# Output projection two steps later, in the batch's own bank, and both rope parts together

## The chip, the cores and the metric

One NeuronCore of one Trainium2 chip. The metric is device time in microseconds of one launch; the kernel before was timed in three runs.

## The reference

Sixteen batches of 128 tokens, 256 features. First cross-attention with 32 heads of 8 features, then a mixture-of-experts block. Cut to what matters here:

```
xn   = layernorm(x)
q    = rope(xn @ Wq, pos);  k = rope(ctx @ Wk, pos);  v = ctx @ Wv     # rope: x1*cos - x2*sin, x1*sin + x2*cos
w    = softmax(q k^T / sqrt(8)) per head                               # 128 x 128 per head
x    = x + (w v) @ Wout + bout
x    = x + moe(layernorm(x))                                           # router, 32 experts, shared expert
```

## The kernel before

Each engine has its own hand-written queue of instructions, and semaphores tie them together. The attention stage is software-pipelined over batches: every engine runs a function `period(b)` for b from -3 to 16 (`periods`, L239; ten of them, b = 2 to 11, in a loop of five turns with two periods in each), and a period has eight steps g = 0 to 7, one for each group of four heads ("quad"). In period b the engines work on batch b and also on b+1, b+2, b+3 (earlier stages) and on b-1, called `o` (the last stages). In the code `m1 = b+1`, `m3 = b+3` and so on. "Batch b" below, of a period, means period(b).

What happens to a batch, in the order of the data:

- `transpose_xc`, `project_k`, `project_q` (TensorE, steps 0 to 2 of the period three earlier) put queries and keys into bank M1. VectorE applies rope: `rope_cos` (L472) multiplies by the cosines, `rope_sin` (L479) by the sines in two instructions. GpSimd adds the two and splits the result into two half-precision parts (`split`). `transpose_k` and `transpose_q` turn them; ScalarE copies them out.
- `logits_q` (L583): one quad of scores with queries on the partitions, into one of two banks SB. VectorE takes the row maximum (`row_max`, L487). After each two quads `transpose_max` (L593) turns the maxima, VectorE copies them (`evac_max`, L494), and a DMA of SyncE writes them into spare rows of `qst` (L309). It is there three steps later that they are needed.
- `logits_k` (L597): the same scores with keys on the partitions and the maximum subtracted by the matmul; on every second step it waits for that DMA. ScalarE takes the exponential (L384). SyncE also copies the keys (`kz`, L302) once ScalarE has done the previous batch's last exponential, ahead of the first DMA of maxima of the period in its queue.
- `weigh_values` (L608): multiplies with the values, into the batch's output bank `OB[par]` (par is the batch's parity). Quads 0 to 3 run at step 4 of the batch's own period, quads 4 to 7 at step 0 of the next.
- In the next period: ScalarE copies the outputs (`evac_OT`, step 2), TensorE turns them (`transpose_outputs`, step 3), VectorE divides by the sums (`normalise`, L500, step 3), TensorE turns the result (`transpose_attn`, L626, step 4) into the right half of bank M0, ScalarE copies it (L412, step 5), TensorE multiplies with Wout (`project_out`, L633, step 6) into the left half of M0, and VectorE adds it to X (L516, step 7) and takes the statistics for the second norm (L529).

Bank M0 is shared: `project_v` and `transpose_q` of later batches write it too, and so `project_v` waits for the X add of an earlier batch and `transpose_attn` waits until the queries are copied out.

At the attention stage's end ScalarE and VectorE also split the shared expert's weights into two parts (L162 in period 14, step 7; L166 in period 15, step 7). During the loop ScalarE issues loads of expert weights, at steps 1, 4 and 6.

Of the kernel before, what the change touches and what calls it, by code (L numbers as in the profile page):

```python
# [26 lines left out]
ALU = mybir.AluOpType  # L27
# [144 lines left out]
def attention(nc, sem, X, identf, st2, ring, ahead, x, ctx_in, pos, wq, wkv, wout, bout):  # L172
    with ExitStack() as es:
# [65 lines left out]
        def periods(eng, period):  # L239

            for n in range(-3, 2):
                period(Batch(n // 2, n % 2))
            with eng.Fori(0, 5) as i:
                for u in range(2):
                    period(Batch(i, 2 + u))
            for n in range(12, NB + 1):
                period(Batch(n // 2, n % 2))

        def inside(b, lo=0, hi=NB - 1):

            return not isinstance(b.n, int) or lo <= b.n <= hi
# [102 lines left out]
        def _(act):  # L356
# [21 lines left out]
            def period(b):  # L378
                m1, m2, m3, m4, o = b + 1, b + 2, b + 3, b + 4, b + -1
                for g in range(QUADS):  # L380
# [26 lines left out]
                    if g == 7 and isinstance(b.n, int) and b.n == 14:  # L407
                        ahead.split_hi(act, raw_wsg)
                    if g == 5 and inside(o):
                        act.wait_ge(attnT_mm, o.n + 1)  # L410
                        at_least(act, wo_mm, o.n)
                        act.copy(attnT[:, :, :], M0[:, D:2 * D].rearrange("p (c t) -> p c t", c=DK)).then_inc(attnT_ok, 1)  # L412
                    if g == 6 and inside(m2):
# [13 lines left out]
        def _(dve):  # L427
# [82 lines left out]
            def period(b):  # L510
                m1, m3, o = b + 1, b + 3, b + -1
                for g in range(QUADS):
                    if g == 7 and inside(o):
                        dve.wait_ge(wo_mm, o.n + 1)
                        dve.wait_ge(x_biased, o.n + 1)
                        dve.tensor_tensor(X[:, o.n, :], M0[:, 0:D], X[:, o.n, :], ALU.add).then_inc(x1_ok, 1)  # L516
                    if g == 3 and inside(m3):
                        rope_cos(m3)
                    if g % 2 == 1:
                        who, half = (b, (g + 3) // 2) if g < 5 else (m1, (g - 5) // 2)  # L520
                        if inside(who):
                            evac_max(who, half)
                    who, u = (b, g + 5) if g < 3 else (m1, g - 3)
                    if inside(who):
                        row_max(who, u)
                    if g == 7 and inside(o):
                        dve.wait_ge(x1_ok, o.n + 1)
                        dve.wait_ge(rope_tab, 3)
                        dve.bn_stats(st2[:, o.n, :], X[:, o.n, :]).then_inc(st2_ok, 1)  # L529
                    if g == 3 and inside(o):  # L530
                        normalise(o)
                    if g == 4 and inside(m3):
                        rope_sin(m3)
                    if g == 4 and isinstance(b.n, int) and b.n == -3:
                        split(dve, m3)
                    if g == 4 and isinstance(b.n, int) and b.n == -2:
                        statistics(4, NB, 1)
                    if g == 7 and isinstance(b.n, int) and b.n == 15:
                        ahead.split_lo(dve, raw_wsg)
# [4 lines left out]
        def _(pe):  # L544
# [34 lines left out]
            def project_v(m):  # L579
                at_least(pe, x1_ok, m.n - 2)  # L580
                pe.matmul(M0[:, 0:D], xcT[m.par][:, DK, :], WKV[:, D:2 * D], start=True, stop=True).then_inc(v_mm, 1)
# [26 lines left out]
            def weigh_values(m, g):  # L608
                pe.wait_ge(exp_ok, QUADS * m.n + g + 1)
                if g == 0:  # L610
                    at_least(pe, v_ok, m.n + 1)
                    at_least(pe, attn_ok, m.n - 1)
                for j in range(4):
# [12 lines left out]
            def transpose_attn(m):  # L626
                pe.wait_ge(attn_ok, m.n + 1)
                pe.wait_ge(qst_ok, min(m.n + 3, NB) if isinstance(m.n, int) else m.n + 3)
                for c in range(DK):
                    ins = pe.transpose(M0[:, D + c * P:D + c * P + P], attn[:, c * P:c * P + P], identf[:, :])  # L630
                ins.then_inc(attnT_mm, 1)

            def project_out(m):  # L633
                pe.wait_ge(attnT_ok, m.n + 1)
                for c in range(DK):
                    ins = pe.matmul(M0[:, 0:D], attnT[:, c, :], WO[:, c, :], start=(c == 0), stop=(c == DK - 1))
                ins.then_inc(wo_mm, 1)
# [3 lines left out]
            def period(b):  # L641
                m1, m2, m3, o = b + 1, b + 2, b + 3, b + -1
                for g in range(QUADS):
# [9 lines left out]
                    if g == 0 and inside(m1):  # L653
                        project_v(m1)
                    if g == 0 and inside(o):
                        for q in range(4, QUADS):
                            weigh_values(o, q)
# [11 lines left out]
                    if g == 3 and inside(o):  # L669
                        transpose_outputs(o)  # L670
                    if g == 4 and inside(o):
                        transpose_attn(o)
                    if g == 5 and inside(m2):
                        transpose_k(m2)
                    if g == 6 and inside(o):
                        project_out(o)
            periods(pe, period)
# [621 lines left out]
```

## Time and profile before

| | us |
|---|---|
| median of three runs (lowest, highest) | 409.04 (405.89, 412.06) |
| the profiled execution | 406.55 |
| its span, first to last instruction | 404.8 |
| busy in the span: TensorE matmul / weight load | 311.9 / 209.2 |
| busy: VectorE, ScalarE, GpSimd | 218.0, 194.0, 165.5 |
| attention stage, about | 0 to 219.7 |

The page cuts the span into 40 slices of about 10 us; the attention stage is the first 22. Times in the rows below are microseconds from the first instruction. Matmuls are pipelined: a row's length reaches past the point at which the next may start, so work on TensorE is best measured from one start to the next.

### The profile page before, as it was taken

The numbers are of one execution on the slowest core, as the hardware profiler recorded it, in microseconds if no ns is written. First come the engines' busy times: TensorE is split into PE (matmuls) and PEld (weight loads), VectorE is DVE, ScalarE is ACT, GpSimd is POOL, SyncE is SP. The second block draws the span as 40 slices with busy tenths as digits, with TensorE's granted clock in tenths as the row PEclk, the third lists the DMA queues.
The fourth block names the chain that finished last, engine by engine and source line by source line (L and its number), as shares of the span: only waits on it lengthen the run. The fifth ranks groups of instructions, "written<-read, shape, count | busy, mean of one in ns | idle before, by whom it ended". The sixth has DMA issues, their size and how long they took to land. (4 is left out here: it accounts for less than half of the span.)

```text
span 404.8 us, 9209 instructions
## 1 busy us (share of the span) xinstructions
PE 311.9 (77%) x2986; PEld 209.2 (52%) x2986; DVE 218.0 (54%) x598; ACT 194.0 (48%) x370; POOL 165.5 (41%) x249
## 2 busy tenths in 40 slices
PE   0668999999999999999884879789888995864000
PEld 0446777767676777776562334546467442331000
DVE  4495777777776777777655358996114321111000
ACT  3136786777677776776663745432324221110000
POOL 4453444433344444332002002545872245777620
PEclk9986999999999999999997599999999999895555
DMA  6311114444355344432100361111337793222265
GB/s 186 133 33 35 36 52 116 126 123 117 107 135 140 102 129 127 130 73 86 42 2 0 132 225 71 28 52 59 98 101 220 219 274 52 24 28 27 25 111 105
DMA packets 35035, 39.27 MB, mean 97 GB/s; under 512 B 8032, under 2 KB 29120, under 8 KB 34752
## 3 DMA queue, kind: packets, MB, share of 16 engines
q1 hardware_dynamic: 24082, 21.55, 18.4%
q10 hardware_dynamic: 8030, 11.93, 10.4%
q0 software_dynamic: 2896, 5.44, 8.0%
q8 instruction: 15, 0.25, 0.2%
q14 instruction: 12, 0.10, 0.1%
HBM read 26.36 MB, written 10.32 MB: 91 GB/s over the span
## 5 line engine op out<-in xcount | busy, mean ns | idle before, releaser
L384 ACT ACTIVATE pw<-bank 128x512 f32<-128x512 f32 x128 | 76.7, 600 | 45.4 <-PE bank L615 34.2
L491 DVE TENSOR_REDUCE mx<-bank 128x4 f16<-128x512 f32 x128 | 87.2, 684 | 16.2 <-PE bank L591 15.4
L261 POOL TENSOR_TENSOR rot<-t 128x256 f32<-128x256 f32 x30 | 21.2, 726 | 93.3 <-DVE t L484 93.3
L604 PE MATMUL bank<-qst,kz 128*128 128x128 f16 x512 | 50.0, 221 | 4.0 <-DMA qst<-mxs 3.3
L591 PE MATMUL bank<-kz,qst 128*128 128x512 f16 x128 | 49.5, 388 | 1.5 <-issue 0.9
L604 PEld LDWEIGHTS bank<-qst,kz 128*128 128x128 f16 x512 | 37.4, 99 | 16.7 <-DMA qst<-mxs 5.3
L615 PE MATMUL bank<-pw,V 128*32 128x128 f32 x1024 | 34.7, 276 | 0.0
L893 POOL DMA_INDIRECT out<-ac,dst x16 | 21.7, 1355 | 27.4 <-DVE ac L1116 10.4
L1173 PE MATMUL mbank<-hT,WSG 128*128 128x512 f16 (+1 forms) x144 | 31.9, 379 | 0.0
L1116 DVE TENSOR_SCALAR ac<-mbank,wpair 128x256 f32<-128x256 f32 x16 | 7.7, 484 | 43.4 <-DMA odd<-ac,dst 40.5
L615 PEld LDWEIGHTS bank<-pw,V 128*32 128x32 f32 x1024 | 25.9, 109 | 9.0 <-issue 7.4
L1185 PE MATMUL mbank<-WSD,ac 128*128 128x256 f32 (+1 forms) x96 | 21.9, 382 | 5.8 <-POOL ac L852 4.4
L498 DVE COPY mxs<-bank 8x128 f16<-8x128 f16 x64 | 13.2, 206 | 23.7 <-PE bank L595 23.7
L852 POOL TENSOR_TENSOR ac<-ac,sg 128x512 f32<-128x512 f32 (+1 forms) x9 | 11.8, 1317 | 34.2 <-ACT ac L933 34.1
L893 POOL DMA_INDIRECT odd<-ac,dst x16 | 21.7, 1354 | 8.1 <-DVE ac L1116 5.9
L1173 PEld LDWEIGHTS mbank<-hT,WSG 128*128 128x128 f16 (+1 forms) x144 | 15.1, 106 | 15.6 <-ACT ac L933 0.4
L1185 PEld LDWEIGHTS mbank<-WSD,ac 128*128 128x128 f32 (+1 forms) x96 | 17.9, 189 | 9.6 <-POOL ac L852 5.4
L272 POOL TENSOR_TENSOR tokst<-rot,tokst 128x256 f16<-128x256 f32 x30 | 20.2, 672 | 4.4
L417 ACT COPY kT<-bank 128x1024 f16<-128x1024 f16 x16 | 16.2, 1011 | 9.8 <-PE bank L576 8.7
L1242 PE MATMUL mbank<-ring_gu,xbT 128*64 128x352 f32 x112 | 18.9, 460 | 0.8 <-ACT xbT L791 0.8
L972 ACT ACTIVATE ac<-mbank 128x176 f32<-128x176 f32 x16 | 5.1, 318 | 29.7 <-PE mbank L1242 27.9
L562 PE MATMUL bank<-WQ,xcT 128*128 128x256 f32 x64 | 18.8, 422 | 0.0
(174 smaller groups left out, 597.3 us busy)
## 6 DMA issues: line engine op xcount, KB each, us to landing
ring_gu<-in_L_ffn_w_gate_up ACTq DMA_DIRECT2D x20, 352.0 KB
kz<-kT SPq DMA_DIRECT2D x64, 64.0 KB, 2.0
ring_dn<-in_L_ffn_w_down ACTq DMA_DIRECT2D x10, 352.0 KB
ring_gu<-in_L_ffn_w_gate_up SPq DMA_DIRECT2D x8, 352.0 KB
X<-in_x SPq DMA_DIRECT2D x4, 512.0 KB, 7.4
table<-ac SPq DMA_DIRECT2D x8, 256.0 KB, 2.2
odd<-zero SPq DMA_DIRECT2D x1, 2048.0 KB, 7.2
out<-X SPq DMA_DIRECT2D x4, 512.0 KB
```

The lines of the kernel that those rows point to most:

```text
L261: eng.tensor_tensor(rot[:, part], t1[:, part], t2[:, part], ALU.add).then_inc(rot_ok[w], 1)
L272: eng.tensor_tensor(tokst[m.par][:, w, :, a:a + HD], r, hi, ALU.subtract)
L384: act.activation(pw[g % 4][:, :], STB[g % 2][:, :], ACT.Exp, scale=SCALE).then_inc(exp_ok, 1)
L491: dve.tensor_reduce(mx[u // 2 % 2][:, u % 2:8:2], SB[u % 2][:, :].rearrange("p (j t) -> p j t", j=4), axis=AX.X, op=ALU.max, negate=True). ...
L562: ins = pe.matmul(M1[:, 0:D], xcT[m.par][:, c, :], WQ[:, c, :], start=(c == 0), stop=(c == DK - 1))
L591: pe.matmul(SB[u % 2][:, :], qst[m.par][:, u, :], kz[m.par][:, :, u, :], start=True, stop=True).then_inc(s_mm, 1)
L604: ins = pe.matmul(STB[g % 2][:, j * P:j * P + P], kz[m.par][:, j, g, :], qst[m.par][:, g, :], start=True, stop=True)
L615: ins = pe.matmul(OB[m.par][32 * j:32 * j + 32, (g % 4) * P:(g % 4) * P + P], V[m.par][:, a:a + SLOT], pw[g % 4][:, j * P:j * P + P], star ...
L893: pool.indirect_dma_start(to[:, :], bass.IndirectOffsetOnAxis(ap=dst[:, 2 * k + w:2 * k + w + 1], axis=0), ys[k % 3][rows, :], None, compu ...
L1173: ins = pe.matmul(GU[2 * (i % 2) + w][0:n, :], WSG[:, c, u, w * SHARED + a:w * SHARED + a + n], hT[:, v, c, 512 * k:512 * k + 512], start= ...
L1185: ins = pe.matmul(DN[m % 2][:, 0:D], ac[k % 2][0:n, f, j * P:j * P + P], WSD[0:n, f, :], start=(f == 0), stop=(f == 2))
L1242: ins = pe.matmul(EB[k % 3][lane, 0:2 * INNER], xbT[:, c, e * CAP:e * CAP + LANE], ring.gu[place][:, e % 2, c, :], start=(c == 0), stop=(c ...
```

## The change

- VectorE: `rope_cos` and `rope_sin` run one behind the other at step 3, after that step's copy of maxima and row maximum. Before, the cosine part came ahead of both and the sine part at the end of step 4.
- VectorE: `normalise` moves from step 3 to step 5.
- TensorE: `transpose_attn` moves from step 4 to step 6, ScalarE's copy of it from step 5 to 7, `project_out` from step 6 to step 0 of the next period, the X add with the statistics from step 7 to step 2 of the next. They write and read the batch's own output bank and no longer M0.
- Waits: `transpose_attn` no longer waits for the copied queries; `project_v` waits for the queries and no longer for the X add; the first `weigh_values` of a batch waits for the X add of the batch two before, where it waited for that batch's normalise.
- One more period (b = 17) runs, for the last batch.

```diff
-            for n in range(12, NB + 1):
+            for n in range(12, NB + 2):
                 period(Batch(n // 2, n % 2))
...
-                    if g == 5 and inside(o):
+                    if g == 7 and inside(o):
                         act.wait_ge(attnT_mm, o.n + 1)
                         at_least(act, wo_mm, o.n)
-                        act.copy(attnT[:, :, :], M0[:, D:2 * D].rearrange("p (c t) -> p c t", c=DK)).then_inc(attnT_ok, 1)
+                        act.copy(attnT[:, :, :], OB[o.par][:, D:2 * D].rearrange("p (c t) -> p c t", c=DK)).then_inc(attnT_ok, 1)
...
             def period(b):
-                m1, m3, o = b + 1, b + 3, b + -1
+                m1, m3, o, o2 = b + 1, b + 3, b + -1, b + -2
                 for g in range(QUADS):
-                    if g == 7 and inside(o):
-                        dve.wait_ge(wo_mm, o.n + 1)
-                        dve.wait_ge(x_biased, o.n + 1)
-                        dve.tensor_tensor(X[:, o.n, :], M0[:, 0:D], X[:, o.n, :], ALU.add).then_inc(x1_ok, 1)
-                    if g == 3 and inside(m3):
-                        rope_cos(m3)
                     if g % 2 == 1:
...
                         row_max(who, u)
-                    if g == 7 and inside(o):
-                        dve.wait_ge(x1_ok, o.n + 1)
+                    if g == 2 and inside(o2):
+                        dve.wait_ge(wo_mm, o2.n + 1)
+                        dve.wait_ge(x_biased, o2.n + 1)
+                        dve.tensor_tensor(X[:, o2.n, :], OB[o2.par][:, 0:D], X[:, o2.n, :], ALU.add).then_inc(x1_ok, 1)
+                        dve.wait_ge(x1_ok, o2.n + 1)
                         dve.wait_ge(rope_tab, 3)
-                        dve.bn_stats(st2[:, o.n, :], X[:, o.n, :]).then_inc(st2_ok, 1)
-                    if g == 3 and inside(o):
+                        dve.bn_stats(st2[:, o2.n, :], X[:, o2.n, :]).then_inc(st2_ok, 1)
+                    if g == 3 and inside(m3):
+                        rope_cos(m3)
+                        rope_sin(m3)
+                    if g == 5 and inside(o):
                         normalise(o)
-                    if g == 4 and inside(m3):
-                        rope_sin(m3)
...
             def project_v(m):
-                at_least(pe, x1_ok, m.n - 2)
+                at_least(pe, qst_ok, m.n)
...
                 if g == 0:
                     at_least(pe, v_ok, m.n + 1)
-                    at_least(pe, attn_ok, m.n - 1)
+                    at_least(pe, x1_ok, m.n - 1)
...
             def transpose_attn(m):
                 pe.wait_ge(attn_ok, m.n + 1)
-                pe.wait_ge(qst_ok, min(m.n + 3, NB) if isinstance(m.n, int) else m.n + 3)
                 for c in range(DK):
-                    ins = pe.transpose(M0[:, D + c * P:D + c * P + P], attn[:, c * P:c * P + P], identf[:, :])
+                    ins = pe.transpose(OB[m.par][:, D + c * P:D + c * P + P], attn[:, c * P:c * P + P], identf[:, :])
...
-                    ins = pe.matmul(M0[:, 0:D], attnT[:, c, :], WO[:, c, :], start=(c == 0), stop=(c == DK - 1))
+                    ins = pe.matmul(OB[m.par][:, 0:D], attnT[:, c, :], WO[:, c, :], start=(c == 0), stop=(c == DK - 1))
...
+                    if g == 0 and inside(o2):
+                        project_out(o2)
                     if g == 0 and inside(o):
                         for q in range(4, QUADS):
                             weigh_values(o, q)
...
-                    if g == 4 and inside(o):
-                        transpose_attn(o)
                     if g == 5 and inside(m2):
                         transpose_k(m2)
                     if g == 6 and inside(o):
-                        project_out(o)
+                        transpose_attn(o)
```

## Rows read from the trace of the kernel before

**Rows 1.** Busy time by stretch, batch 6's period: us and (instructions) of each engine.

```profile
102.01:113.79 11.78, 11.00 (x147) 8.46 (x146) 8.44 (x20) 8.44 (x15) 4.99 (x10) 1.00 0.43 113
```

**Rows 2.** Timeline, TensorE, period 6: start, length, engine, line, operation, [idle before].

```profile
101.56 0.39 PE L604 MATMUL bank<-qst,kz 128*128 128x128 f16 x4 [0.17 <-issue]
...
108.51 0.40 PE L604 MATMUL bank<-qst,kz 128*128 128x128 f16 x4 [0.74 <-DMA qst<-mxs]
...
110.57 0.22 PE L595 MATMUL bank<-identh,mx 128*128 128x128 f16 x1
...
112.65 0.39 PE L604 MATMUL bank<-qst,kz 128*128 128x128 f16 x4
...
113.14 0.39 PE L604 MATMUL bank<-qst,kz 128*128 128x128 f16 x4
```

**Rows 3.** Timeline, TensorE, period 7, up to the next period's first logits.

```profile
117.36 0.38 PE L591 MATMUL bank<-kz,qst 128*128 128x512 f16 x1
...
121.09 0.43 PE L630 MATMUL bank<-identf,attn 128*128 128x128 f32 x2
...
121.61 0.23 PE L595 MATMUL bank<-identh,mx 128*128 128x128 f16 x1
...
122.27 0.62 PE L576 MATMUL bank<-identh,tokst 128*128 128x128 f16 x8 [0.19 <-DVE t L484]
...
123.17 1.03 PE L636 MATMUL bank<-WO,attnT 128*128 128x256 f32 x4
...
124.03 0.39 PE L604 MATMUL bank<-qst,kz 128*128 128x128 f16 x4
...
124.85 0.39 PE L604 MATMUL bank<-qst,kz 128*128 128x128 f16 x4 [0.17 <-issue]
```

**Rows 4.** Timeline, SyncE's queue, period 6: key copy and first DMA of maxima.

```profile
102.64 2.46 SPq L302 DMA_DIRECT2D kz<-kT  x4
...
105.24 0.59 SPq L309 DMA_DIRECT2D qst<-mxs  x1
```

**Rows 5.** Timeline, VectorE: a copy of period 6, then period 7.

```profile
110.92 0.21 DVE L498 COPY mxs<-bank 8x128 f16<-8x128 f16 x1 [0.40 <-PE bank L595]
...
117.78 0.69 DVE L491 TENSOR_REDUCE mx<-bank 128x4 f16<-128x512 f32 x1 [0.61 <-PE bank L591]
...
118.75 0.69 DVE L477 TENSOR_TENSOR t<-bank,RC 128x512 f32<-128x512 f32 x1 [0.28 <-PE bank L562]
...
119.36 0.20 DVE L498 COPY mxs<-bank 8x128 f16<-8x128 f16 x1
...
120.53 0.42 DVE L507 TENSOR_TENSOR attn<-bank,rec 128x256 f32<-128x256 f32 x1
...
120.87 0.68 DVE L491 TENSOR_REDUCE mx<-bank 128x4 f16<-128x512 f32 x1
...
121.47 0.75 DVE L484 TENSOR_TENSOR t<-bank,RS 128x256 f32<-128x256 f32 x2
```

**Rows 6.** Timeline, period 8: DMA of maxima and the logits that waited for it.

```profile
134.28 0.53 SPq L309 DMA_DIRECT2D qst<-mxs  x1
...
136.38 0.40 PE L604 MATMUL bank<-qst,kz 128*128 128x128 f16 x4
```

**Rows 7.** Timeline, end of the attention stage.

```profile
204.41 1.37 ACT L162 ACTIVATE WSG<-raw_wsg 128x1408 f16<-128x1408 f32 x1
...
212.60 1.18 PE L615 MATMUL bank<-pw,V 128*32 128x128 f32 x32
...
212.71 0.60 ACT L384 ACTIVATE pw<-bank 128x512 f32<-128x512 f32 x1 [0.94 <-PE bank L604]
...
213.85 0.59 ACT L422 COPY OT<-bank 128x512 f32<-128x512 f32 x1 [0.55 <-PE bank L615]
```

**Rows 8.** Line L581 (project_v): what TensorE waited for before it (nothing), and who waited.

```profile
its engine sat idle before it (us, times) until:
who waited for it (us, times):
```

More of the change, by code:

```diff
@@ L641, in period @@
             def period(b):
-                m1, m2, m3, o = b + 1, b + 2, b + 3, b + -1
+                m1, m2, m3, o, o2 = b + 1, b + 2, b + 3, b + -1, b + -2
                 for g in range(QUADS):
```

## The prediction

> **What bounds the kernel now.** I read the page's slices first: TensorE, VectorE and ScalarE are all busy and TensorE's clock is full from about 40 to 210 us, which is the attention stage; everything the diff touches lies there or in its last 10 us. The view by stretches then gives one period (one batch): of 11.78 us TensorE's rows cover 11.00, VectorE's and ScalarE's 8.44 each [rows 1]. So TensorE's queue is nearly full, and a period is its work plus the few waits in it. The timeline of TensorE shows where they are. I follow three points of a period: Z, the first key-major logits of step 0; S7, the last query-major logits (step 2); and T, the transpose of the maxima at step 5. In the period from Z 101.56 the queue stood 0.74 at step 4, for the DMA of the maxima; T came at 110.57 and the next Z at 113.14: 11.58 us [rows 2]. In the next period Z to S7 is 4.22, S7 to T 4.25, T to Z 3.24, together 11.71 [rows 3]. Its waits: the transposes of attn start 0.14 after normalise ends (120.53 + 0.42, then 121.09), T starts 0.06 after the row maximum of 120.87 ends, the key transposes wait 0.19 for the sine part, and the last logits stand 0.82 before the next Z, against 0.49 in the period before (112.65 to 113.14) [rows 2, 3, 5]. Every second period ends one turn of the loop, and I take this 0.33 as its price, since nothing in the change touches it.
>
> So the bound is a ring over engines, not one engine: logits, row maximum (VectorE), transpose, copy, DMA, logits three steps later. The question for each moved piece is whether it stood in a wait of that ring and where it stands now.
>
> **The change, part by part.**
>
> 1. *project_out to step 0.* Four matmuls; from their start to the following logits 0.86 (123.17 to 124.03) [rows 3]. At step 6 they filled time between T and Z; at step 0 they stand between Z and S7. That stretch of 4.22 contains no wait of note: the value product beside it waits for an exp that is done long before. Z to S7 becomes 5.08.
>
> 2. *The DMA wait at step 4.* It goes. SP issued the key copy 1.08 after Z, the maxima 2.60 after that, and they were there 3.27 later (102.64, 105.24, 108.51) [rows 2, 4]: 6.95 after Z. TensorE by itself was there at 6.95 − 0.74 = 6.21, and with 0.86 more at 7.07. The wait is covered, in every second period; this is the real gain of the change, 0.74 per pair. The issues on SP's queue stay in their order, and the exp that releases the key copy still ends about half a microsecond after Z. ScalarE's and POOL's DMAs are not reordered either.
>
> 3. *VectorE between S7 and T.* T needs the row maximum of step 4. Before, VectorE did after S7: maximum, (wait), cosine, copy, maximum, reciprocal and normalise, maximum. Now it does: maximum, X add, statistics, copy, maximum, cosine, sine, maximum. Start to start, a maximum takes 0.60 (120.87 to 121.47), the cosine 0.61, copy + maximum + reciprocal 1.17 together (119.36 to 120.53), the normalise 0.34; the sine pair is 0.75 long and I take 0.66 as the others also overlap by 0.09; the last maximum counts 0.69 to its end [rows 5]. X add and statistics are not shown side by side; as 128x256 operations they lie between 0.34 each (normalise's spacing) and 0.46 each (add and release); I take 0.78 for both, because the statistics wait for the add. With 0.42 from S7 to its maximum (117.36 to 117.78), 0.20 at most for the copy and 0.06 to T: 0.42 + 0.60 + 0.78 + 0.20 + 0.60 + 0.61 + 0.66 + 0.69 + 0.06 = 4.62, say 4.6 [rows 3, 5]. TensorE needs less: 4.25 − 0.14 and less the attn transposes that leave step 4 (at most 0.43, their row), so 3.7 to 4.1. VectorE sets T: 4.6. Before it was 4.25 in one period and held by the DMA in the other. The late T holds everything behind it on TensorE: logits, key transposes, logits of steps 6 and 7.
>
> 4. *Between T and Z.* After T VectorE copies (110.57 to 110.92: 0.35), then maximum (+0.13), then 1.04 to normalise, which is 0.42 long, and 0.14 to the attn transposes: T + 2.08 [rows 2, 3, 5]. TensorE would be there some 1.2 us after T and stands; behind the waiting transposes are the logits of step 7. From the attn transposes to the next transpose of maxima took 0.52 with one logits group between (121.09 to 121.61), and logits of step 7 to Z 0.49, of which 0.22 lies before that transpose: Z = T + 2.08 + 0.52 + 0.27 = T + 2.87. The other path to Z is the DMA of the maxima: copy ended 0.56 after T, issue, and 2.10 from issue to logits in a period where TensorE stood for it (134.28 to 136.38) [rows 6]: T + 2.68. So taking 0.86 of work out of this stretch gives nothing back: 2.87 against 2.57 in rows 2 and 3.24 (with the turn) in rows 3.
>
> 5. *Sine behind cosine.* The key transposes no longer wait (0.19 to 0.48 in every second period), and POOL starts its rotation earlier, which nobody waits for. It is contained in 4: they follow T.
>
> 6. *Bank, waits.* The output bank's owner now keeps it until the X add of step 2; the next user comes at step 4, VectorE's add is done about 1 us after S7. Cost nothing; if the add came later, the value products of step 4 and exps 4 to 7 would.
>
> Period: 5.08 + 4.60 + 2.87 = 12.55; a pair 25.10 + 0.33 = 25.43 against 23.29: +2.1. Batches 2 to 11 are five pairs: +10.7, batch 12 +1.0. Batch 1 has no project_out and no add (+0.3), batches 13 and 14 have no rope (+0.9 and, with half of it in waits, +0.4).
>
> 7. *The end.* ScalarE's split of shared weights (204.41, 1.37 long) now stands ahead of the attnT copy, TensorE waits for that at step 0, and its value products, and exp 0 behind them, come after. Exp 0 used to follow the split at once; now copy 0.4, project_out 0.9 and the first value products 0.5 come between, so it is 1.8 later. Without project_out and its wait inside batch 15 about 1.3 comes back. Then the last exp used to be followed by the copy of the outputs at once (213.31, 213.85); now copy 0.4, project_out 0.9 and the whole value product 1.1 come between: +1.9 [rows 7]. Sum +2.4.
>
> Total 10.7 + 1.0 + 0.3 + 0.9 + 0.4 + 2.4 = +15.7 on the profiled run's 406.55, so **422**. That run (span 404.8, 1.75 around it) lies 2.5 under the median of the three runs, 409.04, and inside their range.
>
> **A rule against the trace.** The waits for the shared bank that the change removes are not to be seen: project_v, which waited for the X add, has no row of idle time before it in 16 batches [rows 8]. The Trainium skill, Perfetto Trace Analysis (Optimizing Tensor Performance, Matmuls), says that independent groups of matmuls should rotate through different PSUM banks so that the evacuation of one overlaps the next; by that rule the move into the batch's own bank should pay. Here the evacuations overlap already.
>
> **The rivals.**
> *Faster.* TensorE's waits vanish and no new one comes: S7 to T 3.84 (4.25 less 0.14 and 0.27); T to Z less by 0.59 (out 0.86, in 0.27), so 1.98, and 2.22 with the turn and without the sine's wait of 0.4. Periods of 10.9 and 11.1, a pair 1.25 less, five and a half pairs 6.9: about 400 with the end hidden. For it: TensorE is the fullest engine and the waits at step 4 are real. Against: the DMA's 2.68. It decides if Z follows T by less than 2.4. Chance 0.07. The rule on PSUM banks in the Trainium skill, Perfetto Trace Analysis (Matmuls), would end here.
> *No change.* VectorE's chains don't bind, only the DMA does: 5.08 + 3.84 + 2.68 = 11.60, a pair 23.2 against 23.29, and the end's 2.4: 408.5. Chance 0.14.
> *Only the second chain.* X add and statistics find idle time, so S7 to T is 3.9 rather than 4.6: 0.7 less in twelve periods, 414. Chance 0.14.
> *Worse.* The maxima for Z meet a weight load on the DMA engines and take 3.27 as in rows 4: Z = T + 3.9, 1 us more per period, 433. Against: these loads are issued more than 1 us before them at step 4. Chance 0.05.
>
> **How the numbers follow.** Forecast 0.60, own range 417 to 427 (the chain 4.5 to 4.7, the end 0 to 4). Adding 414 and part of the no-change case: **409 to 427**. A measurement of this kernel can tell about 2%, so faster is below 401, slower above 417: faster 0.07, slower 0.66, the rest 0.27.
>
> **What would show it.** Right: no idle time before the logits of step 4; a new wait of TensorE for VectorE's row maximum before T (about 0.6) and one for normalise before the attn transposes (about 0.9), in each period; periods of 12.4 to 12.9. Wrong: TensorE starts T before the maximum of step 4 would be ready by 3, or waits for the DMA at Z.

## The result: 425.89 us, 4.6% slower

The changed kernel took **425.89 us** (median of four runs, 423.59 to 426.62) against 407.47 for the kernel before (four runs, 405.28 to 412.06): ratio 1.046, 95% interval 1.038 to 1.054. The forecast was 422, range 409 to 427. A few runs fall into a slower state, and the ratios here and below leave these out, so they can lie some tenths of a per cent off the quotient of the medians. The profiled execution took 426.11 with a span of 424.4, 19.6 more than the 404.8 before. TensorE's row in the page is 316.5 us busy; more time, with the same work in it:

```profile
PE 316.5 (75%) x2986; PEld 211.1 (50%) x2986; DVE 218.7 (52%) x598; ACT 193.4 (46%) x370; POOL 164.2 (39%) x249
```

Periods 6 and 7 of the changed kernel in the view by stretches (length, then for PE, PEld, DVE, ACT, POOL busy us and count, granted clock, DMA share, GB/s), the counterpart of [rows 1]:

```profile
105.92:118.44 12.52, 11.12 (x145) 8.64 (x146) 8.26 (x19) 8.04 (x15) 4.36 (x10) 1.00 0.38 105
118.44:131.39 12.95, 11.30 (x146) 8.55 (x145) 8.95 (x21) 8.87 (x17) 5.22 (x10) 1.00 0.42 112
```

TensorE's rows still cover 11.1 and 11.3 us of a period at full clock; the periods around them have grown from 11.6 and 11.7 to 12.5 and 12.95. The waits of TensorE between 60 and 180 us in the changed kernel (waiting line, releaser: total us, times, longest) say what fills the gap:

```profile
PE bank L627 <- DVE attn L507: 6.6, 9, 0.7
PE bank L593 <- DVE mx L491: 6.6, 10, 0.7
PE bank L602 <- ACT pw L384: 1.1, 4, 0.3
PE bank L589 <- DMA kz<-kT: 0.3, 1, 0.3
```

The same view of the kernel before, between 60 and 170 us:

```profile
PE bank L604 <- DMA qst<-mxs: 3.3, 5, 0.7
PE bank L576 <- DVE t L484: 0.9, 5, 0.2
```

Both old waits are gone, the DMA's and the sine part's, 4.2 us together. Two new ones, 13.2 us together, stand in nearly every period: the transpose of the maxima (now line 593) waits for VectorE's row maximum, and the transposes of attn (now 627) for normalise. Here they are in TensorE's timeline of period 7, with Z at 118.44, S7 at 123.33, T at 127.98 and the next Z at 131.39 (start, us, row; in brackets the idle time before it and its releaser), beside [rows 3]:

```profile
118.44 0.39 PE L602 MATMUL bank<-qst,kz 128*128 128x128 f16 x4
...
123.33 0.38 PE L589 MATMUL bank<-kz,qst 128*128 128x512 f16 x1
...
125.36 0.39 PE L602 MATMUL bank<-qst,kz 128*128 128x128 f16 x4
...
127.98 0.23 PE L593 MATMUL bank<-identh,mx 128*128 128x128 f16 x1 [0.67 <-DVE mx L491]
...
130.06 0.44 PE L627 MATMUL bank<-identf,attn 128*128 128x128 f32 x2 [0.73 <-DVE attn L507]
...
131.39 0.40 PE L602 MATMUL bank<-qst,kz 128*128 128x128 f16 x4 [0.26 <-ACT pw L384]
```

The logits of step 4 (125.36) have no idle time before them. VectorE in the same period, beside [rows 5]:

```profile
123.75 0.69 DVE L491 TENSOR_REDUCE mx<-bank 128x4 f16<-128x512 f32 x1 [0.61 <-PE bank L589]
124.36 0.41 DVE L523 TENSOR_TENSOR X<-bank,X 128x256 f32 x1
124.92 0.43 DVE L526 BATCH_NORM_STATS2 st<-X  x1
125.27 0.20 DVE L498 COPY mxs<-bank 8x128 f16<-8x128 f16 x1
125.39 0.67 DVE L491 TENSOR_REDUCE mx<-bank 128x4 f16<-128x512 f32 x1
125.98 0.67 DVE L477 TENSOR_TENSOR t<-bank,RC 128x512 f32<-128x512 f32 x1
126.58 0.73 DVE L484 TENSOR_TENSOR t<-bank,RS 128x256 f32<-128x256 f32 x2
127.25 0.67 DVE L491 TENSOR_REDUCE mx<-bank 128x4 f16<-128x512 f32 x1
...
129.58 0.42 DVE L507 TENSOR_TENSOR attn<-bank,rec 128x256 f32<-128x256 f32 x1
```

From 123.75 to 127.92 the one gap is the 0.15 in which the statistics wait for the X add (124.77 to 124.92). Otherwise VectorE runs without a pause up to the maximum that T waits for, and T starts 0.06 after that has ended.

**Where the 19.6 us went** (differences between the two profiled executions, from Z of one period to Z of another): start to Z of batch 2 −0.35; batches 2 to 11 +11.56 (116.15 to 127.71); batch 12 +0.92; batch 13 +0.87; batch 14 +0.60; from Z of batch 15 to the end of attention +5.98 (15.75 to 21.73). They sum to 19.58; after attention nothing changed.

### The profile page after: what moved, and what is told of

Its sections match the earlier page's. It is cut to its first block and busy times, and to the rows that moved or that the text cites. A ratio compares the mean times of both kernels' runs of the same rounds, so it can differ in the third digit from the quotient of the medians.

```text
span 424.4 us, 9203 instructions
## 1 busy us (share of the span) xinstructions
PE 316.5 (75%) x2986; PEld 211.1 (50%) x2986; DVE 218.7 (52%) x598; ACT 193.4 (46%) x370; POOL 164.2 (39%) x249
## 5 line engine op out<-in xcount | busy, mean ns | idle before, releaser
L491 DVE TENSOR_REDUCE mx<-bank 128x4 f16<-128x512 f32 x128 | 87.0, 687 | 13.3 <-PE bank L589 12.9
L1182 PE MATMUL mbank<-WSD,ac 128*128 128x256 f32 (+1 forms) x96 | 23.6, 403 | 5.4 <-POOL ac L849 4.0
L849 POOL TENSOR_TENSOR ac<-ac,sg 128x512 f32<-128x512 f32 (+1 forms) x9 | 11.7, 1304 | 33.8 <-ACT ac L930 33.7
L593 PE MATMUL bank<-identh,mx 128*128 128x128 f16 x64 | 14.5, 227 | 13.7 <-DVE mx L491 13.0
L1182 PEld LDWEIGHTS mbank<-WSD,ac 128*128 128x128 f32 (+1 forms) x96 | 19.0, 201 | 9.7 <-POOL ac L849 5.0
L633 PE MATMUL bank<-WO,attnT 128*128 128x256 f32 x64 | 18.7, 419 | 2.7 <-ACT attnT L412 2.7
```

The costliest lines, as they stand in the source:

```text
L491: dve.tensor_reduce(mx[u // 2 % 2][:, u % 2:8:2], SB[u % 2][:, :].rearrange("p (j t) -> p j t", j=4), axis=AX.X, op=ALU.max, negate=True). ...
L633: ins = pe.matmul(OB[m.par][:, 0:D], attnT[:, c, :], WO[:, c, :], start=(c == 0), stop=(c == DK - 1))
L1182: ins = pe.matmul(DN[m % 2][:, 0:D], ac[k % 2][0:n, f, j * P:j * P + P], WSD[0:n, f, :], start=(f == 0), stop=(f == 2))
```

## The experiments

The table gives the stretches between the three points of the prediction for all kernels (Z, the first key-major logits of step 0; S7, the last query-major logits; T, the transpose of the maxima at step 5): means over periods 4 to 10 (even) and 3 to 11 (odd, with the turn of the loop), in us, each from the kernel's own profile.

| kernel | even: Z–S7, S7–T, T–Z | odd: Z–S7, S7–T, T–Z | pair | ratio of times (95%) |
|---|---|---|---|---|
| before | 4.04, 4.92, 2.64 | 4.17, 4.25, 3.18 | 23.19 | 1 |
| changed | 4.89, 4.64, 3.00 | 4.89, 4.64, 3.38 | 25.43 | 1.046 (1.038–1.054) |
| bank_only | 4.02, 4.71, 2.69 | 4.20, 4.25, 3.22 | 23.07 | 1.002 (0.997–1.006) |
| rope_only | 4.02, 5.28, 2.55 | 4.22, 5.27, 2.84 | 24.19 | 1.022 (1.016–1.029) |
| out_only | 4.89, 4.33, 2.89 | 4.89, 4.25, 3.19 | 24.44 | 1.024 (1.017–1.031) |
| rope_back | 4.89, 4.35, 2.98 | 4.89, 4.35, 3.35 | 24.81 | 1.032 (1.026–1.039) |
| x_early | 4.88, 4.49, 3.00 | 4.89, 4.48, 3.37 | 25.12 | 1.036 (1.029–1.043) |
| norm4 | 4.89, 4.64, 2.50 | 5.21, 4.64, 2.84 | 24.73 | 1.028 (1.020–1.036) |
| split_last | 4.90, 4.64, 2.99 | 4.89, 4.64, 3.36 | 25.44 | 1.036 (1.029–1.043) |
| load_step2 | 4.02, 4.34, 2.99 | 4.22, 4.25, 3.17 | 22.99 | 1.000 (0.996–1.003) |
| mended | 4.88, 4.49, 2.50 | 5.23, 4.48, 2.86 | 24.44 | 1.022 (1.016–1.027) |
| norm_next | 4.05, 4.03, 2.89 | 4.05, 4.26, 2.78 | 22.05 | 0.982 (0.976–0.987) |
| norm_next1 | 4.05, 4.66, 2.87 | 4.06, 4.14, 2.83 | 22.60 | 0.995 (0.991–0.998) |

For rope_only, out_only, mended and norm_next the interval shows that there is a difference, but not whether it is more than 2%.

The first four are the parts of the change, one each, or all but one.

**bank_only**: the kernel before, with the outputs' transposes and projection in the batch's own bank, everything in its old step.

```diff
-                    ins = pe.transpose(M0[:, D + c * P:D + c * P + P], attn[:, c * P:c * P + P], identf[:, :])
+                    ins = pe.transpose(OB[m.par][:, D + c * P:D + c * P + P], attn[:, c * P:c * P + P], identf[:, :])
...
-                    ins = pe.matmul(M0[:, 0:D], attnT[:, c, :], WO[:, c, :], start=(c == 0), stop=(c == DK - 1))
+                    ins = pe.matmul(OB[m.par][:, 0:D], attnT[:, c, :], WO[:, c, :], start=(c == 0), stop=(c == DK - 1))
```

> The kernel before with one part of the change alone: the output transposes, their copy, the output projection and the X add use the batch's own output bank, with the waits of the changed kernel, but stay in their old steps. Theory (a ring over TensorE, VectorE and the DMA of maxima sets the period; where a piece stands counts, not its bank): no change, 406.5 to 408.5 against 407.5 before, periods 11.5 to 11.8 us. Rival (groups in rotating banks free TensorE): 404 or less. Rival (the output bank is fuller and its users get in each other's way, which would be the cause of the slower kernel): 412 or more.

Measured: 407.02 (12 runs) against 406.54, no difference. Its waits of TensorE between 60 and 170 us are those of the kernel before, with a single one of 2.0 for a copy of the keys in addition:

```profile
PE bank L591 <- DMA kz<-kT: 2.0, 1, 2.0
PE bank L604 <- DMA qst<-mxs: 1.9, 4, 0.6
PE bank L576 <- DVE t L484: 0.9, 5, 0.2
```

So the bank itself is worth nothing here, for or against, as far as the interval of half a per cent to either side can tell. The Trainium skill, Perfetto Trace Analysis (Optimizing Tensor Performance, Matmuls), says that independent matmul groups should rotate through different PSUM banks, so that the evacuation of one overlaps the next; no gain from it shows in this kernel. The whole loss lies in the steps to which the work was moved.

**rope_only**: the kernel before with cosine and sine together behind the maximum of step 3.

```diff
-                    if g == 3 and inside(m3):
-                        rope_cos(m3)
                     # (row_max and the rest of the step)
+                    if g == 3 and inside(m3):
+                        rope_cos(m3)
+                        rope_sin(m3)
-                    if g == 4 and inside(m3):
-                        rope_sin(m3)
```

> The kernel before with the rope part alone: cosine and sine one behind the other at step 3, behind the copy of maxima and the row maximum; normalise follows them, still at step 3. Theory: from S7 (last query-major logits) to T (transpose of maxima, step 5) 0.42 + wait for the copy 1.25 + copy 0.13 + maximum 0.60 + cosine 0.61 + sine 0.66 + reciprocal 0.44 + normalise 0.34 + maximum 0.75 = 5.2 us in every period, against 4.25 and 5.0 before; the key transposes no longer wait for the sine. A pair of periods costs 0.8 more, 5.5 pairs 4.4: 412. Rival (the sine's place is harmless and its wait of TensorE was a loss): 404 to 407.

Measured: 414.65 (before 406.54), 2.2% slower, with S7–T at 5.28 and 5.27. VectorE in its period 6:

```profile
111.33 0.75 DVE L484 TENSOR_TENSOR t<-bank,RS 128x256 f32<-128x256 f32 x2
112.00 0.34 DVE L504 RECIPROCAL rec<-bank 128x32 f32<-128x32 f32 x1
...
112.79 0.68 DVE L491 TENSOR_REDUCE mx<-bank 128x4 f16<-128x512 f32 x1
```

The sine part costs 0.67 (111.33 to 112.00) in front of the maximum that T needs. It saves 0.2 us of wait in front of the key transposes in every second period and puts 1.02 in front of T in the same period.

**out_only**: the other half, projection and X add moved, rope and normalise as before.

```diff
-                    if g == 6 and inside(o):
-                        project_out(o)
+                    if g == 0 and inside(o2):
+                        project_out(o2)
```

(with the X add and its statistics behind the maximum of step 0 of that period, and the bank of bank_only)

> The kernel before with the output projection alone moved to step 0 of the next period, in the output bank; the X add and the statistics follow it at step 0, where VectorE is idle, so that its chain between S7 and T is as before; rope, normalise and the transposes of attn stay in their steps. Theory: Z to S7 4.89 (0.87 more), S7 to T 4.25, T to Z limited by the DMA of maxima at 2.8 to 3.1 although TensorE has 0.87 less to do there: mean period 12.0 to 12.2 against 11.65, 12 periods 4 to 7 more, the end 1.5 more: 413 to 416. Rival (all of the cost of the change is VectorE's longer chain; the place of the projection is worth nothing): 407 to 409.5.

Measured: 414.70, 2.4% slower. Z–S7 is 4.89 in each period. In odd periods that is 0.72 more than before, in even ones 0.85. T–Z, out of which the same work was taken, is 2.89 and 3.19, against 2.64 and 3.18. T (111.28 in this period) has no wait; what stands is the next transpose of maxima, that of step 7, 0.3 ahead of Z. It waits in every period for the maximum (113.11 to 113.80) of step 6's logits:

```profile
113.86 0.23 PE L594 MATMUL bank<-identh,mx 128*128 128x128 f16 x1 [0.56 <-DVE mx L491]
```

With the 0.28 that the key transposes stand for the sine part before it, that is 0.84 of waiting between T and Z, about as much as was taken out.

**rope_back**: the changed kernel with cosine and sine at their old places.

```diff
+                    if g == 3 and inside(m3):
+                        rope_cos(m3)
                     # (row_max and the rest of the step)
-                    if g == 3 and inside(m3):
-                        rope_cos(m3)
-                        rope_sin(m3)
+                    if g == 4 and inside(m3):
+                        rope_sin(m3)
```

> The changed kernel with only the rope parts put back (cosine at the start of step 3, sine at the end of step 4). Theory: S7 to T falls from 4.64 to 3.9, where TensorE's own work sets it; the sine then stands before the copy of maxima, so T to Z grows from 2.99 to 3.2; mean period 12.1 to 12.3 against 12.73, in all 5 to 7 less than the changed kernel's 425.9: 419 to 421. Rival (the rope parts' place is worth nothing, the rest of the change is the cost): 425 to 427. Rival (the rope order is all of the cost): 410 or less.

Measured: 418.58, 0.9% above out_only (414.70) and 3.2% above the kernel before. S7–T is 4.35, not the 3.9 expected. An edge that I had left out shows in its TensorE row:

```profile
123.13 0.39 PE L590 MATMUL bank<-kz,qst 128*128 128x512 f16 x1 [0.36 <-DVE mxs L498]
```

The query-major logits of step 4 go into the bank from which VectorE copies the transposed maxima, and that copy now stands behind X add and statistics. So the X add does cost in front of T, if by another edge. T–Z is 2.98 rather than 3.2, and the two misses cancel in part.

The next four change one suspected cost each.

**x_early**: the changed kernel with X add and statistics two steps earlier.

```diff
-                    if g == 2 and inside(o2):
+                    if g == 0 and inside(o2):
```

> The changed kernel with the X add and its statistics at step 0 instead of step 2 (VectorE is idle there for 2.3 us). VectorE has the same work per period. Theory (only the chain from S7 to T counts, and taking 0.8 out of it leaves the wait for the transposed maxima of step 3): copy starts at S7 + 1.67, then 0.13 + 0.60 + 0.61 + 0.66 + 0.75 to T = 4.42 instead of 4.64; T to Z unchanged at 3.0: 12 periods of 0.2, 2.6 less than the changed kernel: 423. Rival (the add and the statistics cost their full length in every period): S7 to T 3.86, 416.5. Rival (VectorE's total load is what counts): 426.

Measured: 423.24 (before 407.16). S7–T is 4.49 and 4.48, 0.15 less: what VectorE then does between S7 and T is shorter by 0.9, but it waits for the transposed maxima instead. The chain has two nearly equal limbs.

**norm4**: the changed kernel with reciprocal and normalise one step earlier.

```diff
-                    if g == 5 and inside(o):
+                    if g == 4 and inside(o):
```

> The changed kernel with normalise at step 4, behind the row maximum, instead of step 5: TensorE's wait before the transposes of attn (0.7 to 0.9 in each period) goes. Theory: normalise now stands before the copy of maxima, which starts at T + 0.65 instead of T + 0.36; issue and 2.1 to 2.4 of DMA put the next Z at T + 3.0 to 3.3, so T to Z stays at 3.0 or grows by 0.3 and the wait is to be found before the first logits of the next period, for the DMA: 425 to 429. Rival (the wait before the transposes is the cost): T to Z 2.4, 418 to 419.

Measured: 418.78. This one went against my theory: T–Z fell to 2.50 and 2.84, 0.5 less. A wait for the DMA of the maxima did take the place of the one for normalise, but a short one. VectorE's and TensorE's rows at the end of a period of norm4:

```profile
139.65 0.23 PE L593 MATMUL bank<-identh,mx 128*128 128x128 f16 x1 [0.67 <-DVE mx L491]
139.95 0.42 DVE L507 TENSOR_TENSOR attn<-bank,rec 128x256 f32<-128x256 f32 x1
140.30 0.20 DVE L498 COPY mxs<-bank 8x128 f16<-8x128 f16 x1
...
140.84 0.38 PE L627 MATMUL bank<-identf,attn 128*128 128x128 f32 x2
...
142.15 0.23 PEld L602 LDWEIGHTS bank<-qst,kz 128*128 128x128 f16 x4 [0.19 <-DMA qst<-mxs]
142.16 0.40 PE L602 MATMUL bank<-qst,kz 128*128 128x128 f16 x4
142.90 0.38 ACT L412 COPY attnT<-bank 128x256 f32<-128x256 f32 x1
143.34 1.13 PE L633 MATMUL bank<-WO,attnT 128*128 128x256 f32 x4
```

The copy of the maxima ended at 140.50 and the logits that need them started at 142.16, 1.66 later, transfer included. TensorE's weight load for these logits stood 0.19 for the DMA, so the DMA sets Z here, at T + 2.50. The path that I had feared exists, but the 2.10 of [rows 6] is no floor for it. The attn transposes start 0.5 after normalise has ended and wait for nothing. Normalise was what held Z after T in the changed kernel. What is new is the 0.3 in Z–S7 of odd periods (5.21): project_out stands for ScalarE's attnT copy (142.90), which is queued behind exps.

**split_last**: the changed kernel with ScalarE's split of the shared weights in period 14 behind the attnT copy.

```diff
-                    if g == 7 and isinstance(b.n, int) and b.n == 14:
-                        ahead.split_hi(act, raw_wsg)
                     # (the attnT copy)
+                    if g == 7 and isinstance(b.n, int) and b.n == 14:
+                        ahead.split_hi(act, raw_wsg)
```

> The changed kernel with ScalarE's split of the shared weights behind the copy of attnT in period 14 instead of ahead of it. Theory: the output projection of batch 13 starts 1.2 us earlier, TensorE stands less and keeps its full clock there (it was at 0.50 from 219.5 to 223.5): the first exp of batch 15 comes 2.5 us earlier; 2.5 to 4 less in all: 422 to 423.5, and the stretch from the first logits of batch 15 to the end of attention 18 to 19 instead of 21.7. Rival (the end is long because of the added period and the order of the last steps): 425 to 426.

Measured: 422.59. The period is unchanged (25.44 a pair); Z of batch 15 to the end is 17.02, against 21.73 in the changed kernel and 15.75 before. Of these 4.7 us the profiled run shows 2.4 in its span, since its part after the attention stage, which the edit doesn't touch, is 3.0 longer.

**load_step2**: the kernel before with ScalarE's first weight load of a period at step 2 instead of 1, so that it is not in front of the maxima's DMA.

```diff
-                    if g in (1, 4, 6) and not isinstance(b.n, int):
-                        ring.load_first(act, b.n - 2, (1, 4, 6).index(g))
+                    if g in (2, 4, 6) and not isinstance(b.n, int):
+                        ring.load_first(act, b.n - 2, (2, 4, 6).index(g))
```

> The kernel before with the first of ScalarE's three weight loads per period issued at step 2 instead of step 1, so that the maxima of step 1 are no longer behind it on the DMA engines in every second period. Theory: the 0.74 us wait at step 4 goes, but VectorE's chain (normalise, maximum, sine) then holds T and the key transposes as in the other periods: S7 to T 4.25 in all, T to Z 0.3 more; 0.3 to 0.4 per pair, 1.5 to 2 in all: 405 against 407, ratio 0.993 to 0.998. Rival (the wait is a loss of its own): 4 less, ratio 0.990. Rival (it is the key copy's issue on the same queue, not the load): ratio 1.000 and the wait stays.

Measured: 407.23 (12 runs) against 407.16: no difference, not the gain of 0.2 to 0.7% that I expected. The wait at step 4 did go; from its period 6, the maxima's DMA, the weight load now behind it, and the logits of step 4 without idle time:

```profile
103.71 0.60 SPq L309 DMA_DIRECT2D qst<-mxs  x1
104.64 0.44 ACTq L119 DMA_DIRECT2D ring_gu<-in_L_ffn_w_gate_up  x1
...
106.04 0.39 PE L604 MATMUL bank<-qst,kz 128*128 128x128 f16 x4
```

S7–T in even periods fell by 0.58 (4.92 to 4.34) and T–Z grew by 0.35 (2.64 to 2.99): once TensorE is early there, it waits for VectorE behind it. 0.2 per pair is left, 1.1 us over batches 2 to 11, which the interval (0.996 to 1.003) can't tell from nothing. In the profiled run the batches behind the loop gave that back (12 to 14: 35.38 against 33.13), and all of it in batch 14, 13.32 against 11.07. TensorE stood there for 0.57 and for 1.55, and the granted clock was then 0.50, the level of 1.2 GHz, from 197.9 to 201.3:

```profile
197.36 0.38 PE L591 MATMUL bank<-kz,qst 128*128 128x512 f16 x1 [1.55 <-issue]
```

```profile
198.00:201.00 3.00, 3.00 (x39) 1.95 (x37) 1.83 (x4) 0.60 (x1) 0.00 (x0) 0.50 0.00 0
```

Whether other runs of this kernel have this too is not on record. So even the DMA wait, the one true gain of the change, was worth about 1 us.

The last three kernels ask whether the loss can be mended, and what the ring would pay for.

**mended**: x_early, norm4 and split_last together in the changed kernel.

> The changed kernel with three repairs together: X add and statistics at step 0, normalise at step 4, the split of the shared weights behind the copy of attnT. The output projection stays at step 0 and the rope parts stay together. Theory (the terms are separate stretches of one ring and add up, but for the ring's price of the projection's place): S7 to T 4.4 to 4.5, T to Z 2.5, Z to S7 4.9 to 5.2; 418.8 (normalise alone) less 2 and less 3: 413 to 415. Rival (with all waits of VectorE gone the projection's place costs nothing): 407 to 409.

Measured: 417.13 (before 408.12), above the 413 to 415 expected. The repairs don't add up: S7–T takes x_early's −0.15, T–Z takes norm4's −0.5, the wait for attnT in odd periods (5.23) stays, and I had counted the end twice. What is left, 2.2%, is above all the projection between Z and S7: that stretch is 1.90 a pair longer than before, where the whole pair is 1.25 longer.

**norm_next**: built on the kernel before. Normalise goes to step 0 of the following period, where VectorE is not on the way to T. The attn transposes follow at the end of step 2, the attnT copy at 3, project_out at its old step 6 but one batch later, the X add at 7, all in M0; the weight load at step 2. Periods 2 and 3 stand outside the loop.

```diff
-                    if g == 3 and inside(o):
-                        normalise(o)
+                    if g == 0 and inside(o2):
+                        normalise(o2)
...
-                    if g == 4 and inside(o):
-                        transpose_attn(o)
+                    if g == 2 and inside(o2):
+                        transpose_attn(o2)
...
-                    if g == 6 and inside(o):
-                        project_out(o)
+                    if g == 6 and inside(o2):
+                        project_out(o2)
```

> A version meant to beat the kernel before, made from it: bank M0, the sine at step 4 and the projection at step 6 stay; normalise moves to step 0 of the period after (VectorE stands idle there for 1.5 us), the transposes of attn to step 2 and their copy to step 3 of that period, projection and X add at its steps 6 and 7; weight loads at steps 2, 4, 6; periods 2 and 3 are taken out of the loop (four turns). Theory: nothing but row maxima, copy, cosine and sine is left between S7 and T, so S7 to T is 4.1 (TensorE's own work) and the sine is done before the key transposes: T to Z 2.6 to 2.7; periods of 10.8 and 11.2 instead of 11.6; ten of them 6 less, one turn less 0.3, the end 1.5 to 2 more: 401 to 403, ratio 0.985 to 0.99. Rival (ScalarE's exps, dense from step 4 to 7, then set the period): 405 to 407. Rival (a batch more in flight only lengthens the end): 408 to 410.

Measured: **399.96** (six runs) against 408.12, 1.8% faster (0.976 to 0.987), the fastest of all kernels here. Its timeline of TensorE and VectorE in one period:

```profile
100.98 0.38 PE L591 MATMUL bank<-kz,qst 128*128 128x512 f16 x1
...
104.99 0.22 PE L595 MATMUL bank<-identh,mx 128*128 128x128 f16 x1
...
106.23 1.03 PE L636 MATMUL bank<-WO,attnT 128*128 128x256 f32 x4
...
107.78 0.23 PEld L604 LDWEIGHTS bank<-qst,kz 128*128 128x128 f16 x4 [0.36 <-DMA qst<-mxs]
107.79 0.40 PE L604 MATMUL bank<-qst,kz 128*128 128x128 f16 x4
...
109.84 0.42 DVE L507 TENSOR_TENSOR attn<-bank,rec 128x256 f32<-128x256 f32 x1
```

S7 at 100.98, T at 104.99, Z at 107.79. No wait for VectorE is left before S7, T or Z. Z itself is set by the DMA of the maxima: TensorE's weight load for it stood 0.36, which the matmuls before it nearly covered. A period is now 11.0 us, what TensorE's rows cover of one in [rows 1].

**norm_next1**: the same with the weight load back at step 1.

> The same with the weight loads at steps 1, 4, 6 as before. Theory: the maxima of step 1 are again behind a load in some periods; then the wait of 0.7 at step 4 stays in every second period and is now the ring's only one: 3 to 4 more than with the loads at 2, 4, 6, 405 to 406. Rival (the loads' place is worth nothing, as it was in the kernel before): the same time as with 2, 4, 6.

Measured: 405.84 (12 runs), 0.5% faster than before (0.991 to 0.998). Even S7–T is 4.66 again: the DMA wait of [rows 2] is back. The medians of norm_next and norm_next1 are 5.9 us apart, and their intervals don't overlap. The profiles show 2.1 of it, over batches 2 to 11 (112.17 against 110.05), which is mostly the DMA wait; what makes the rest is not shown. In load_step2 the same move of the load was worth next to nothing, since VectorE stood right behind the DMA.

## Why the prediction held, point by point

**Point 1, project_out at step 0: right.** Z to S7 is 4.89 where 5.08 was forecast. The added 0.86 was right in even periods (4.04 to 4.89), but the base of 4.22 came from an odd one, and these grew by 0.72 only (4.17 to 4.89). Before, TensorE's weight load for the query-major logits behind Z stood 0.20 there (at 113.56) for the copy of the maxima, which came behind the X add of step 7; with the X add gone from there, so is this wait. out_only shows the same 4.89 without the rest of the change.

**Point 2, the DMA wait at step 4: right that it goes, but not only by the way forecast.** No row of it is left. The forecast kept the transfer at 3.27 and covered it with 0.86 more of TensorE's work, by a margin of 0.12. In the kernel before, the maxima were issued together with ScalarE's weight load (105.24 and 105.25). In the changed kernel the load comes later by more than the maxima do, and in period 6 these now go 0.48 ahead of it:

```profile
109.99 0.60 SPq L309 DMA_DIRECT2D qst<-mxs  x1
110.47 0.39 ACTq L119 DMA_DIRECT2D ring_gu<-in_L_ffn_w_gate_up  x1
```

The logits of step 4 follow at 112.83, 2.84 after the issue, without a wait; in load_step2, with the load behind the maxima too, they start 2.33 after it without one. So the transfer is not the 3.27 of the forecast, which had taken the order of the issues as unchanged.

**Point 3, VectorE between S7 and T: right.** 4.64 on 4.6, with two small errors that nearly cancel. Term by term from period 7: X add and statistics 0.91 (124.36 to 125.27) where 0.78 was taken, the copy 0.12 where 0.20 was, cosine 0.60, sine 0.67. The rival "only the second chain" (3.9) falls with rope_back too: without the sine part S7–T is still 4.35, by the edge from the copy of the maxima to the logits of step 4, which I had not seen.

**Point 4, T to Z: the size right, one of its two reasons wrong.** The attn transposes came 2.08 after T (127.98 to 130.06), as forecast; T–Z is 3.00 in even periods, for 2.87. "Gives nothing back" holds: the 0.86 taken out of this stretch returned nothing. The second path, for the DMA, was put too late: not at T + 2.68 but at T + 2.50, as norm4 shows, where it sets Z. The transfer took 2.10 in [rows 6], issued 1.1 us behind a weight load, and 1.6 in norm4 with that load 2 us ahead; that the distance is the reason is not shown by a run of its own. The forecast didn't need this path, since normalise's was longer. The argument against the faster rival (Z within 2.4 of T) still holds with 2.50, though by less; the price of the no-change rival was 0.2 a period too high. The better argument against them was VectorE in front of T.

**Point 5, the sine part: right.** The 0.19 to 0.48 in front of the key transposes is gone, and rope_only shows what it was paid with, 1.02 in front of T in odd periods.

**Point 6, the bank: right.** bank_only: 1.002 (0.997 to 1.006).

**The sum over the batches: right.** A pair of periods was forecast at 25.43 and is 25.43; that it fits to the hundredth is luck, since Z–S7 was put 0.38 a pair too long and the rest (S7–T, T–Z, the turn of the loop) as much too short. Batches 2 to 11 came to +11.56 for +10.7 (the pair before was 23.19, not 23.29, and periods 2 and 3 grew by 3.11, more than the 2.24 of a mean pair), batch 12 +0.92 for 1.0, 13 +0.87 for 0.9, 14 +0.60 for 0.4, the start −0.35 for +0.3. Together +13.60 for +13.3.

**Point 7, the end: mis-sized, +5.98 for +2.4.** This one term holds nearly all of the 4 us by which 422 was short. The end of the changed kernel, where ScalarE's split holds the attnT copy and that holds project_out:

```profile
217.89 1.37 ACT L162 ACTIVATE WSG<-raw_wsg 128x1408 f16<-128x1408 f32 x1
219.16 0.36 ACT L412 COPY attnT<-bank 128x256 f32<-128x256 f32 x1
219.57 2.07 PE L633 MATMUL bank<-WO,attnT 128*128 128x256 f32 x4 [1.27 <-ACT attnT L412]
```

The same two stretches by windows (columns as above):

```profile
217.60:219.50 1.90, 0.71 (x6) 0.29 (x4) 1.48 (x3) 1.90 (x3) 0.00 (x0) 0.86 0.01 1
219.50:223.50 4.00, 3.92 (x37) 2.62 (x38) 0.00 (x0) 0.62 (x2) 0.00 (x0) 0.50 0.00 0
```

The order of events is as forecast. But project_out takes 2.07 where it takes 1.03 elsewhere: the granted clock is 0.50, 1.2 GHz instead of 2.4, from 219.0 to 225.8 us. It fell while TensorE stood for 1.27 (218.30 to 219.57). x_early has the same wait at the same place and keeps the full clock:

```profile
219.29 1.13 PE L633 MATMUL bank<-WO,attnT 128*128 128x256 f32 x4 [1.27 <-ACT attnT L412]
```

```profile
219.20:223.20 4.00, 3.56 (x51) 2.42 (x51) 2.19 (x5) 2.04 (x5) 0.00 (x0) 1.00 0.02 4
```

Its Z of batch 15 to the end is 18.16, or +2.41: the forecast term, without the fall of the clock. Its parts fit too: exp 0 comes 1.91 later than before (1.8 forecast), 1.15 comes back inside batch 15 (1.3), and from the last exp to the copy of the outputs it is 1.98 longer (1.9); 0.34 comes back behind that, which the forecast had not. rope_back and norm4, with the same order of steps at the end and full clock until 230.5, have 18.3. So the fall cost some 3.6 us in the profiled run (21.73 − 18.16). That it hits most runs of the changed kernel I can only infer: of its four runs the shortest, 423.59, has the highest mean clock (0.921, the others 0.907 to 0.916), which is weak, as the clock falls in other stages too. What decides whether the clock falls there stays open.

**The rivals.** None of them came. The kernel that did come out faster, norm_next, shows what the faster rival would have needed: not a free bank, but VectorE's chains out of S7–T and T–Z.

## What to carry to other kernels

Where a period is a ring over several engines (here logits, row maximum, transpose, copy, DMA, logits), split it at two or three marks on the fullest queue and ask of each moved piece in which stretch it stood and in which it stands now. Filler that leaves a stretch set by another engine's latency gives back nothing, and the same filler put in a stretch that its own queue sets costs its length, less the waits that it covers or removes there: 0.86 us of matmuls moved that way cost 2.4% without any new work. What pays is the reverse, moving the side work of the late engine into a stretch where nobody waits for it, which here was worth 1.8% together with the placing of a weight load, and 0.5% without it. That placing had been worth next to nothing by itself.

## What the hardware showed beside this

- A small transfer of the maxima between on-chip buffers is no constant: TensorE waited for it until 1.6 us after its issue with the last weight load issued 2 us ahead (norm4, even periods), until 2.0 to 2.1 with the load 1.1 ahead ([rows 6] and two more periods of the kernel before), and until 3.27 with a weight load issued at the same time [rows 4].
- Equal idle times of TensorE (1.27 us, same place) were followed by the 1.2 GHz level in one profiled run (after) and by full clock in another (x_early). The level of 1.2 GHz also followed a wait of 2.01 us in bank_only (granted clock 0.52 from 61.2 to 64.6) and waits of 0.57 and 1.55 in load_step2 (0.50 from 197.9 to 201.3).
- The turn of the loop costs about 0.4 us a pair in the changed kernel (T–Z 3.38 against 3.00); in norm_next, where the DMA sets Z in most periods, nothing of it can be seen (2.78 with the turn, 2.89 without).
